# An attention and FFN layer on one core: the residual's DMA transposes move from ScalarE's queue to the sync queue

## The chip, the cores and the metric

One core of a Trainium2 chip runs the whole layer in one launch. The metric is the device time of one execution in microseconds; lower is better. Five engines run their own programs in order and meet through semaphores: TensorE (PE), VectorE (DVE), ScalarE (ACT), GpSimd (POOL) and SyncE (SP). DMAs are issued here by SP and by ACT, each from its own queue, in the order of its program.

## The reference

```python
def reference(x, wq, bq, wk, bk, wv, bv, wl, bl, w1, w2, w3):   # x: (1, 2048, 1024) f32
    h = layernorm(x)
    q, k, v = (h @ w.T + b for each of the three, as (S, 32 heads, 32))
    scores = einsum('bshd,bstd->bsht', q, k) / sqrt(32)     # over the heads of ONE token
    x = x + einsum('bsht,bstd->bshd', softmax(scores), v)
    h = layernorm(x)
    dq1, dq2, dq3 = nf4_quant_dequant(w1), ...(w2), ...(w3)   # w1, w2: (2752, 1024), w3: (1024, 2752)
    return x + (silu(h @ dq1.T) * (h @ dq2.T)) @ dq3.T
```

Attention mixes the 32 heads within each token, so each token has its own 32x32 score matrix. The latent projection of the original is computed there and not used. nf4_quant_dequant rounds each weight, divided by the largest magnitude of its block of 64, to one of 16 levels.

## The kernel before, in words

The tokens are cut into T = 16 tiles of 128. The first 105 us or so load and split the three projection weights into two f16 halves (wT_hi, wT_lo). Then the attention runs as a software pipeline of steps n = 0 to 15, and from about 570 us the FFN takes over. Steps 2 to 13 are a hardware loop of six rounds with two steps each, u = 0 for even n and u = 1 for odd n. Steps 14 and 15 are written out, and a tail finishes the last two tiles while the FFN's first units begin ("feed").

In step n the work of three tiles is mixed. Tile n is projected to q, k and v. Tile n-1 gets its attention: its scores are 64 small f32 matmuls between the projection's matmuls of 512 columns, with the block-diagonal q_diag as weights, and its mix is another 64, with p_diag as weights. Tile n-2 gets its end: context, residual, second norm and transpose.

PE in step n: the first projection with the scores (project_one with score_part), the turn of tile n+1, the second projection, and the third with the mix (mix_part) inside its last half. 24 matmuls of 512 columns carry the scores, 16 carry the mix. score_part waits for q_placed, k_ready and ctx_read: the last says that weigh has read the previous context out of the two banks that scores and context share.

VectorE in step n (step at line 755): weigh(n-2), which waits for the mix; one evacuation; the statistics; flip_context; turn_v; norm_apply; look 1; moments2; two evacuations; center (the row maximum of the scores); norm2; the low half of the turned x; flip_probs; the row sums; look 2; the transpose of q; look 3; an evacuation; look 4; an evacuation; the transpose of k; look 5; the last evacuation. A "look" (look_at, L752) takes the block maxima of one 512 KB slice of an FFN weight in ff_raw, which has two slots. A step with u = 0 has five looks, one with u = 1 has four, step 14 has six, step 15 none. The list for a step is `todo`, and SP loads by the same list.

The part that the change touches is the end of tile n-2:

1. VectorE: norm2 writes the normed rows into x_res (L857).
2. ScalarE: halve2 writes the f16 high half to x2_half (L952), after the previous tile's two transposes (x2_turned).
3. A DMA transpose, x2_half to x2_hi (turn_high2, L597). It also waits until the previous tile's x2_hi and x2_lo are stored (x2_out).
4. POOL: low2 writes the f16 low half into x2_half (L709), once that transpose has landed.
5. A DMA transpose, x2_half to x2_lo (turn_low2, L602), after low2 (x2_lo_done).
6. SP: store_x2 stores both to DRAM (L649), once both have landed. load_res loads the next tile's rows into x_res (L255) after low2.

SP's program for a step is: load_x (L252); the first load of todo (load_ff, L611 or L613); store_x1 (L643), which waits for POOL's residual; loads 2 to 4 of todo; load_res after low2; the loads from the fifth on (`todo[4:]`); store_x2. Each load_ff waits until the look two loads earlier has freed its slot of ff_raw (for the first of each round, until the look just before). In step 15 SP also issues the loads of the FFN's first weights, after parts of the projection.

ScalarE's program for a step is: split_hi, exponential, halve2, turn_high2, place_probs (four copies that make p_diag, L908), turn_low2, place of q_diag (four copies). In the tail the transposes of the last two tiles are issued by SP already.

Of the kernel before, what the change touches and what calls it, by code (L numbers as in the profile page):

```python
# [182 lines left out]
def attention(nc, g):  # L183
# [13 lines left out]
    with ExitStack() as mine:  # L197
# [53 lines left out]
        def load_x(sp, n, slot):  # L251
            sp.dma_start(x_nat[:, slot], x_dram[bass.ds(n * P, P), :]).then_inc(x_in[slot], 16)  # L252

        def load_res(sp, n):
            sp.dma_start(x_res[:], x_dram[bass.ds(n * P, P), :]).then_inc(res_in, 16)  # L255
# [265 lines left out]
        projected = sem("projected")  # L521
# [59 lines left out]
        def looks(n, u, it):  # L581

            if it is not None:
                places = [u * IN_LOOP[0] + k for k in range(IN_LOOP[u])]
                return [(it * 3 + 2 + q // 3, q % 3, it * 9 + 6 + q, P, q % 2, it * (5, 4)[q % 2] + 3 + q // 2 + 1, 1 + (q == 0))
                        for q in places]
            if n < 2:
                return [(j // 3, j % 3, j, P, j % 2, j // 2 + 1, 1) for j in range(3 * n, 3 * n + 3)]
            first = 6 + 9 * LOOP
            return [(j // 3, j % 3, j, P if j < 3 * FT else REST, (j + 1 - first) % 2, (5, 4)[(j + 1 - first) % 2] * LOOP + 3 + (j - first) // 2 + 1, 1)  # L590
                    for j in range(first, first + 6)] if n == T - 2 else []

        def turn_high2(eng, n):
            eng.wait_ge(x2_out, 32 * (n + 1))
            eng.wait_ge(x2_hi_done, n + 1)
            eng.sem_inc(held, 1)
            eng.dma_start_transpose(x2_hi[:], x2_half[:]).then_inc(x2_turned, 16)  # L597

        def turn_low2(eng, n):
            eng.wait_ge(x2_lo_done, n + 1)  # L600
            eng.sem_inc(held, 1)
            eng.dma_start_transpose(x2_lo[:], x2_half[:]).then_inc(x2_turned, 16)  # L602

        def sync(sp, feed):
            def load_ff(tile, m, j, rows, slot, times, behind):
                first = tile * P
                sp.wait_ge(absmax_done, j + behind)
                if m == 2:
                    sp.sem_inc(held, 1)
                if m < 2:  # L610
                    sp.dma_start(ff_raw[0:rows, slot], (w1, w2)[m][bass.ds(first, rows), :]).then_inc(ff_in[slot], 16)  # L611
                else:
                    sp.dma_start(ff_raw[:, slot, 0:C * rows].rearrange("p (t h) -> p t h", t=C),  # L613
                                 w3.rearrange("(t p) h -> p t h", p=P)[:, :, bass.ds(first, rows)]).then_inc(ff_in[slot], 16)

            def step(n, u, it, project=True, normalize=True, attend=True, end=True, feed=None):
                todo = looks(n, u, it)
                if normalize and not (it is None and n + 2 >= T):
                    sp.wait_ge(x_turned, 2 * n + 2)
                    load_x(sp, n + 2, u)  # L620
                for look in todo[:1]:
                    load_ff(*look)
                if end:
                    store_x1(n - 2)
                if feed:
                    sp.wait_ge(projected, 6 * n + 2)
                    next(feed)
                for look in todo[1:4]:
                    load_ff(*look)
                if end and attend:  # L630
                    sp.wait_ge(x2_lo_done, n - 1)
                    load_res(sp, n - 1)
                if feed:
                    sp.wait_ge(projected, 6 * n + 4)
                    next(feed)
                for look in todo[4:]:
                    load_ff(*look)
                if end:
                    store_x2(n - 2)

            def store_x1(n):
                sp.wait_ge(res_done, n + 1)
                sp.dma_start(x1_dram[bass.ds(n * P, P), :], x_res[:]).then_inc(x1_out, 16)  # L643

            def store_x2(n):
                sp.wait_ge(x2_turned, 32 * (n + 1))
                sp.sem_inc(held, 1)
                for dram, part in ((x2_hi_dram, x2_hi), (x2_lo_dram, x2_lo)):
                    sp.dma_start(dram[bass.ds(n * P, P), :], part[:].rearrange("p c s -> p (c s)")).then_inc(x2_out, 16)  # L649

            def tail(feed):
                sp.wait_ge(projected, 6 * T)
                sp.wait_ge(evacuated, 6 * T)
                sp.wait_ge(x2_out, 32 * (T - ST_BLOCK + 1))
                next(feed)
                store_x1(T - 2)
                sp.wait_ge(q_placed, T)
                sp.wait_ge(v_ready, T)
                sp.wait_ge(x2_turned, 32 * (T - 2))
                next(feed)  # L660
                next(feed)
                turn_high2(sp, T - 2)
                sp.wait_ge(x2_lo_done, T - 1)
                load_res(sp, T - 1)
                turn_low2(sp, T - 2)
                store_x2(T - 2)
                next(feed)
                store_x1(T - 1)
                next(feed)
                next(feed)  # L670
                turn_high2(sp, T - 1)
                turn_low2(sp, T - 1)
                store_x2(T - 1)

            sp.wait_ge(projected, 1)
            load_res(sp, 0)
            sp.sem_inc(x2_out, 32)
            all_steps(sp, step, tail, feed)
            sp.wait_ge(x1_out, 16 * T)
            sp.wait_ge(x2_out, 32 * (T + 1))  # L680
# [223 lines left out]
        def scalar(act, feed):  # L904
            def place(diag, compact, done):

                for rows in quadrants:
                    last = nc.scalar.activation(diag[rows, :, rows], compact[rows].rearrange("p (t h) -> p t h", h=HEADS), ACT.Copy)  # L908
                last.then_inc(done, 1)

            def step(n, u, it, project=True, normalize=True, attend=True, end=True, feed=None):
                if normalize:
                    split_hi(act, n + 1, xT_hi[:, 1 - u], x_turned, x_hi_done)
                if attend:
                    exponential(n)
                if end:
                    halve2(n - 2)
                    turn_high2(act, n - 2)
                if attend:
                    place_probs(n, end)  # L920
                if feed:
                    next(feed)
                if end:
                    turn_low2(act, n - 2)
                if project:
                    act.wait_ge(q_ready, n + 1)
                    if attend:
                        act.wait_ge(scores_done, n)
                    else:
                        act.wait_ge(diag_zero, 1)  # L930
                    place(q_diag, qT[:].rearrange("p t h -> p (t h)"), q_placed)
                if feed:
                    next(feed)

            def exponential(n):
                act.wait_ge(centered, n)
                flat = probs[:].rearrange("p t h -> p (t h)")
                nc.scalar.activation(flat, flat, ACT.Exp, scale=float(1 / np.sqrt(np.float32(HD)))).then_inc(exp_done, 1)

            def place_probs(n, end):  # L940
                act.wait_ge(p_ready, n)
                if end:
                    act.wait_ge(context_done, n - 1)
                else:
                    act.wait_ge(diag_zero, 2)
                place(p_diag, flipped[:], p_placed)

            def halve2(n):
                act.wait_ge(normed2, n + 1)
                if not (isinstance(n, int) and n == 0):  # L950
                    act.wait_ge(x2_turned, 32 * n)
                nc.scalar.activation(x2_half[:], x_res[:], ACT.Copy).then_inc(x2_hi_done, 1)  # L952

            def tail(feed):
                next(feed)
                exponential(T)
                next(feed)
                place_probs(T, True)
                next(feed)
                halve2(T - 2)  # L960
                next(feed)
                halve2(T - 1)

            all_steps(act, step, tail, feed)

        def tensor(pe, feed_program):
# [891 lines left out]
```

## Time and profile before

| | |
|---|---|
| median of 3 runs | 2005.99 us (2005.11 to 2007.31) |
| the profiled execution, its own time | 2009.52 us |
| its span in the trace | 2007.6 us |
| mean granted TensorE clock | 0.987 of full speed |
| one loop step (weigh to weigh) | 32.6 us |

The profile is of one execution. Times in rows are us from the start of its span, durations of single instructions are in us in a timeline and in ns where a mean is given. A row of a timeline has the start, the busy time, the engine, the line of the kernel, the operation, and what it writes and reads. "[1.54 <-DMA ff_raw...]" says that the engine stood idle for 1.54 us before it and what ended that. "SPq" and "ACTq" are DMA issues on the queues of SP and ACT; the data lands later. "PEclk" is the granted TensorE clock as a share of 2.4 GHz.

### The profile page before, as it was taken

What the parts mean: (1) busy time and instruction counts of PE and PEld (TensorE: products, weight loads), DVE (VectorE), ACT (ScalarE), POOL (GpSimd) and SP (SyncE); (2) the same over time, 40 slices, a digit from 0 to 9 for tenths busy, and PEclk for the clock granted to TensorE, in tenths of its full rate; (3) what the DMA queues carried; (4) which work ended last, traced back from release to release, by engine and by line L of the source; (5) the groups of instructions that cost most, each with busy time, mean ns of one, the idle gap of its engine ahead of it and who ended that gap; (6) DMA issues with size and microseconds to landing.
All of it is one profiled execution on the core that took longest, in us unless ns stands there. A gap on an engine that the chain in (4) does not pass through costs nothing. (4 is left out here: it accounts for less than half of the span.)

```text
span 2007.6 us, 30891 instructions
## 1 busy us (share of the span) xinstructions
PE 1964.3 (98%) x10444; PEld 1070.1 (53%) x10444; DVE 1784.9 (89%) x1789; ACT 1456.1 (73%) x1592; POOL 1189.5 (59%) x713
## 2 busy tenths in 40 slices
PE   6999999999999989999999999999999999999998
PEld 6678777777775434444444444444444444444442
DVE  6788898989877899999999999999999999999982
ACT  7242424233365889989899898998989989898882
POOL 0111111111133778787787877878778787886974
PEclk9999999999977999999999999999999999999999
DMA  7235555464445632221212122121222212122114
GB/s 304 94 93 158 149 157 162 131 167 141 127 146 153 225 90 59 48 58 42 63 42 63 42 47 57 42 63 42 53 51 45 59 42 63 42 48 53 38 28 177
DMA packets 253418, 183.77 MB, mean 92 GB/s; under 512 B 177456, under 2 KB 220464, under 8 KB 253360
## 3 DMA queue, kind: packets, MB, share of 16 engines
q1 hardware_dynamic: 223792, 175.67, 31.3%
q10 hardware_dynamic: 29568, 7.34, 2.1%
q8 instruction: 34, 0.56, 0.1%
q14 instruction: 24, 0.20, 0.0%
HBM read 115.34 MB, written 25.17 MB: 70 GB/s over the span
## 5 line engine op out<-in xcount | busy, mean ns | idle before, releaser
L1587 DVE SCALAR_TENSOR_TENSOR bank<-signs,bank 128x1024 f32<-128x1024 int8 (+2 forms) x761 | 926.5, 1217 | 53.9 <-ACT signs L1451 25.8
L1451 ACT ACTIVATE signs<-w_nat,compare_bias 128x1024 int8<-128x1024 f32 (+2 forms) x896 | 959.2, 1133 | 5.1 <-POOL w_nat L1335 1.3
L1758 PE MATMUL bank<-x2T_hi,w12T_hi 128*128 128x512 f16 x1376 | 521.5, 379 | 2.1 <-DVE w_nat L1604 1.3
L1759 PE MATMUL bank<-x2T_lo,w12T_hi 128*128 128x512 f16 x1376 | 521.5, 379 | 0.0
L1760 PE MATMUL bank<-x2T_hi,w12T_lo 128*128 128x512 f16 x1376 | 521.5, 379 | 0.0
L985 PE MATMUL bank<-wT_hi,xT_hi 128*128 128x512 f16 x768 | 294.0, 383 | 2.4 <-PEq L324 2.4
L985 PE MATMUL bank<-wT_hi,xT_lo 128*128 128x512 f16 x768 | 294.3, 383 | 0.0
L1785 PE MATMUL bank<-w3T_hi,hT_hi 128*128 128x512 f16 x672 | 255.7, 380 | 8.5 <-DMA w3T_lo<-half 5.8
L1787 PE MATMUL bank<-w3T_hi,hT_lo 128*128 128x512 f16 x672 | 255.4, 380 | 0.0
L1786 PE MATMUL bank<-w3T_lo,hT_hi 128*128 128x512 f16 x672 | 255.3, 380 | 0.0
L1377 POOL TENSOR_TENSOR acc<-acc,hidden 128x512 f32<-128x512 f32 x176 | 221.0, 1270 | 45.7 <-ACT hidden L1500 44.9
L1347 POOL TENSOR_SCALAR step_part<-w_nat 128x1024 f32<-128x1024 f32 (+1 forms) x64 | 230.5, 3602 | 14.3 <-POOL w_nat L1360 7.4
L1758 PEld LDWEIGHTS bank<-x2T_hi,w12T_hi 128*128 128x128 f16 x1376 | 134.6, 98 | 165.1 <-DVE w_nat L1604 1.8
L1760 PEld LDWEIGHTS bank<-x2T_hi,w12T_lo 128*128 128x128 f16 x1376 | 134.6, 98 | 162.4
L1759 PEld LDWEIGHTS bank<-x2T_lo,w12T_hi 128*128 128x128 f16 x1376 | 134.6, 98 | 162.1
L1356 POOL TENSOR_TENSOR w_nat<-w_nat,step_part 128x1024 f32<-128x1024 f32 (+1 forms) x64 | 149.7, 2339 | 101.5 <-DVE w_nat L1587 101.5
L1500 ACT ACTIVATE hidden<-bank,un_scale 128x512 f32<-128x512 f32 x176 | 120.2, 683 | 116.2 <-PE bank L1787 60.7
L290 ACT ACTIVATE xT_hi<-bank 128x512 f16<-128x512 f32 x32 | 17.4, 594 | 245.4 <-PE bank L284 245.4
L274 POOL TENSOR_TENSOR rstd<-var_eps,power 128x1 f32<-128x1 f32 x16 | 8.8, 552 | 275.7 <-DVE var_eps L266 275.7
L1029 PEld LDWEIGHTS bank<-vT,p_diag 128*128 128x128 f32 x1024 | 157.1, 208 | 17.0 <-ACT p_diag L908 8.4
L1666 DVE SCALAR_TENSOR_TENSOR acc<-bank,un_scale,acc 128x512 f32<-128x512 f32 x176 | 131.4, 746 | 38.7 <-PE bank L1783 28.4
L1019 PEld LDWEIGHTS bank<-kT,q_diag 128*128 128x128 f32 x1024 | 156.1, 191 | 11.8 <-issue 0.3
(141 smaller groups left out, 2720.0 us busy)
## 6 DMA issues: line engine op xcount, KB each, us to landing
ff_raw<-in_L_ffn_w SPq DMA_DIRECT2D x63, 512.0 KB, 4.4
w_nat<-in_L_ffn_w SPq DMA_DIRECT2D x63, 512.0 KB, 3.8
x_nat<-in_L_attn_hidden_states SPq DMA_DIRECT2D x16, 512.0 KB, 3.9
x_res<-in_L_attn_hidden_states SPq DMA_DIRECT2D x16, 512.0 KB, 4.9
x<-x_res SPq DMA_DIRECT2D x16, 512.0 KB, 3.0
acc<-x SPq DMA_DIRECT2D x4, 2048.0 KB, 8.7
out<-acc SPq DMA_DIRECT2D x16, 512.0 KB, 2.6
w_raw<-in_L_attn_wq SPq DMA_DIRECT2D x8, 512.0 KB, 7.3
```

The costliest lines, as they stand in the source:

```text
L985: ins = nc.tensor.matmul(to, x, w, start=j == 0, stop=j == len(passes) - 1)
L1029: ins = nc.tensor.matmul(context[:, t], p_diag[:, t], vT[:, t], start=True, stop=True)
L1347: nc.gpsimd.tensor_scalar(step_part[0:rows, 0:cols], w_nat[0:rows, slot, 0:cols], float(BOUNDS[APART]), 2 * HALF_STEP[APART], ALU.is_gt, A ...
L1377: nc.gpsimd.tensor_tensor(acc[:, st, BANK:], acc[:, st, BANK:], hidden[:, st % 2], ALU.add).then_inc(summed, 1)
L1451: nc.scalar.activation(signs[0:rows, ring(v, k), 0:cols], w_nat[0:rows, v % SLOTS, 0:cols], ACT.Sign, scale=COMPARE[SUMMED[k]][0], bias=co ...
L1587: V.scalar_tensor_tensor(to, part, HALF_STEP[SUMMED[k]], before, ALU.mult, ALU.add).then_inc(sign_used, 1)
L1758: nc.tensor.matmul(dst, hi, x2T_hi[:, toks, c], start=c == 0, stop=False)
L1759: nc.tensor.matmul(dst, hi, x2T_lo[:, toks, c], start=False, stop=False)
L1760: last = nc.tensor.matmul(dst, lo, x2T_hi[:, toks, c], start=False, stop=c == C - 1)
L1785: nc.tensor.matmul(dst, hT_hi[k, p, toks], w3T_hi[k, p, cols], start=p == 0, stop=False)
L1786: nc.tensor.matmul(dst, hT_hi[k, p, toks], w3T_lo[k, p, cols], start=False, stop=False)
L1787: last = nc.tensor.matmul(dst, hT_lo[k, p, toks], w3T_hi[k, p, cols], start=False, stop=p == GROUP - 1)
```

## The change

The two DMA transposes of tile n-2 in steps 2 to 15 are no longer issued by ScalarE but by SP. In SP's program the high one stands behind loads 2 to 4 of todo, and the low one behind load_res, ahead of `todo[4:]`. In step 15, where SP also serves the FFN, load_res stands behind the second of the FFN's loads instead of ahead of it. The tail stays as it is, and no computation changes.

```diff
--- before.py
+++ after.py
@@ -627,12 +627,16 @@
                     next(feed)
                 for look in todo[1:4]:
                     load_ff(*look)
+                if end:
+                    turn_high2(sp, n - 2)
+                if feed:
+                    sp.wait_ge(projected, 6 * n + 4)
+                    next(feed)
                 if end and attend:
                     sp.wait_ge(x2_lo_done, n - 1)
                     load_res(sp, n - 1)
-                if feed:
-                    sp.wait_ge(projected, 6 * n + 4)
-                    next(feed)
+                if end:
+                    turn_low2(sp, n - 2)
                 for look in todo[4:]:
                     load_ff(*look)
                 if end:
@@ -915,13 +919,10 @@
                     exponential(n)
                 if end:
                     halve2(n - 2)
-                    turn_high2(act, n - 2)
                 if attend:
                     place_probs(n, end)
                 if feed:
                     next(feed)
-                if end:
-                    turn_low2(act, n - 2)
                 if project:
                     act.wait_ge(q_ready, n + 1)
                     if attend:
```

The two helpers that are called are unchanged:

```python
        def turn_high2(eng, n):
            eng.wait_ge(x2_out, 32 * (n + 1))
            eng.wait_ge(x2_hi_done, n + 1)
            eng.sem_inc(held, 1)
            eng.dma_start_transpose(x2_hi[:], x2_half[:]).then_inc(x2_turned, 16)
```

turn_low2 waits for x2_lo_done alone and writes x2_lo.

## Rows read from the trace of the kernel before

**Rows 1.** The page, busy time and share of the span for each engine.
```profile
PE 1964.3 (98%) x10444; PEld 1070.1 (53%) x10444; DVE 1784.9 (89%) x1789; ACT 1456.1 (73%) x1592; POOL 1189.5 (59%) x713
```

**Rows 2.** Timeline of PE and its weight loads: first of mix, first of scores.
```profile
340.57 0.56 PEld L1029 LDWEIGHTS bank<-vT,p_diag 128*128 128x128 f32 x4 [0.19 <-ACT p_diag L908]
...
351.72 0.30 PE L1019 MATMUL bank<-kT,q_diag 128*128 128x32 f32 x2
```

**Rows 3.** Timeline of VectorE and POOL: looks, low2 and weigh of two loop steps.
```profile
337.27 1.21 DVE L752 TENSOR_REDUCE absmax<-ff_raw 128x1024 f32 x1
338.08 2.13 POOL L709 TENSOR_TENSOR x_half<-x_res,x_half 128x1024 f16<-128x1024 f32 x1 [8.40 <-DMA x_hi<-x_half]
...
342.04 1.22 DVE L752 TENSOR_REDUCE absmax<-ff_raw 128x1024 f32 x1
...
347.46 1.22 DVE L752 TENSOR_REDUCE absmax<-ff_raw 128x1024 f32 x1 [1.54 <-DMA ff_raw<-in_L_ffn_w]
...
350.07 1.23 DVE L829 TENSOR_TENSOR probs<-bank,inv_sum 128x1024 f32<-128x1024 f32 x1 [0.73 <-PE bank L1029]
...
382.70 1.23 DVE L829 TENSOR_TENSOR probs<-bank,inv_sum 128x1024 f32<-128x1024 f32 x1 [2.68 <-PE bank L1029]
...
391.34 1.21 DVE L752 TENSOR_REDUCE absmax<-ff_raw 128x1024 f32 x1
```

**Rows 4.** Timeline of ScalarE in the step of rows 2.
```profile
333.79 1.04 ACT L952 ACTIVATE x_half<-x_res 128x1024 f16<-128x1024 f32 x1
334.92 1.25 ACTq L597 DMA_TRANSPOSE x_hi<-x_half  x1
336.27 4.25 ACT L908 ACTIVATE p_diag<-flipped 32x1024 f32<-32x1024 f32 x4 [1.44 <-DVE flipped L865]
340.31 1.25 ACTq L602 DMA_TRANSPOSE x_lo<-x_half  x1
```

**Rows 5.** Timeline of SP's queue: three loads of the loop, two issues of the tail.
```profile
338.66 0.33 SPq L611 DMA_DIRECT2D ff_raw<-in_L_ffn_w  x1
...
341.43 0.33 SPq L611 DMA_DIRECT2D ff_raw<-in_L_ffn_w  x1
...
381.68 0.35 SPq L611 DMA_DIRECT2D ff_raw<-in_L_ffn_w  x1
...
621.95 0.50 SPq L1245 DMA_DIRECT2D w_nat<-in_L_ffn_w  x1
622.58 1.24 SPq L597 DMA_TRANSPOSE x_hi<-x_half  x1
```

**Rows 6.** DMA issues, last number us to landing: whole kernel, then 615 to 640.
```profile
x_hi<-x_half ACTq DMA_TRANSPOSE x14, 3.1
...
w_nat<-in_L_ffn_w SPq DMA_DIRECT2D x1, 512.0 KB, 4.8
...
x_hi<-x_half SPq DMA_TRANSPOSE x1, 5.0
```

**Rows 7.** Timeline of PE: first matmul of the last two mixes.
```profile
571.40 0.79 PE L1029 MATMUL bank<-vT,p_diag 128*128 128x32 f32 x4 [3.04 <-ACT p_diag L908]
...
615.54 0.41 PE L1029 MATMUL bank<-vT,p_diag 128*128 128x32 f32 x2 [1.92 <-ACT p_diag L908]
```

**Rows 8.** Windows: length, PE busy (matmuls), granted clock, DMA share, GB/s.
```profile
340.70:350.00 9.30, 9.30 (x82) 1.00 0.95 262
351.70:361.90 10.20, 10.20 (x89) 1.00 0.32 107
571.40:588.80 17.40, 17.40 (x79) 0.51 0.45 106
588.80:592.20 3.40, 3.40 (x10) 0.50 0.03 8
615.50:634.70 19.20, 18.38 (x83) 0.52 0.53 110
634.70:640.00 5.30, 5.30 (x15) 0.50 0.73 229
```

## The prediction

> **What bounds the kernel now.** I read the page first, then the timeline of a loop step engine by engine, then PE's waits around the two places where it needs other engines, and last the landing times of the transposes. PE is busy for 98% of the span [rows 1]: whatever makes PE stand is paid in full, and what frees another engine is worth only the standing of PE that it ends.
>
> In a loop step PE runs the scores inside the first projection, then turns x, projects twice more with the mix inside the last half, and goes on to the next step. In the stretches of the mix and of the scores it is busy without a gap [rows 8]. It needs p_diag for the mix, and there the weight load waited 0.19 us for it; it needs weigh(n - 2), which frees the scores' banks, at 351.72, the first score [rows 2].
>
> The margin that matters is VectorE's before that score. weigh starts at 350.07 and lasts 1.23 us, to 351.30: 0.42 us before PE asks. In the steps with u = 0 a fifth look at a slice of FFN weights stands ahead of weigh. It starts at 347.46 after 1.54 us of waiting for its DMA; VectorE then idles 0.73 us before weigh [rows 3]. So that load may land 0.73 + 0.42 = 1.15 us later, at about 348.6, before PE stands. With u = 1 there is no fifth look, and VectorE idles 2.68 us before weigh [rows 3].
>
> **What the change takes from ScalarE.** Two DMA issues of 1.25 us per step [rows 4]. The first stands between x_half and p_diag: p_diag starts at 336.27, the transpose ends at 334.92 + 1.25 = 336.17, and flip_probs ends a little earlier, so I estimate p_diag 0.1 to 0.3 us sooner. PE can get back at most the 0.19 us of the weight load in each of 13 steps, 2.5 us; part of that is covered by the matmul still running. In step 15 PE stands 3.04 us for p_diag [rows 7], and there the transpose costs it up to 1.25 us. The second transpose stands before q_diag, which PE needs only for the next step's scores. Together between 0 and 3.7 us of gain; I take 1, mostly step 15.
>
> **What it does to the sync queue.** SP issues in order. The high transpose now stands behind todo[1:4], the low one behind POOL's low2 and load_res, and todo[4:], the load of that fifth look, behind both. With x_half ready at 334.83 (333.79 + 1.04) [rows 4], a step with u = 0 goes so:
>
> The last load of todo[1:4] is issued at 338.66, after the look at 337.27 has freed its slot [rows 3, 5]. The high transpose follows at about 339.1, not at 334.92. It lands 5.0 us later if it behaves as the SP transpose at 622.58, which also stands 0.6 us behind a 512 KB load; as ScalarE's it would take 3.1 [rows 5, 6]. The situation is that of the row with 5.0, so I take it: 344.1.
>
> POOL's low2 takes 2.13 us [rows 3]: 346.3. Then load_res at 346.4, the low transpose from 346.8 to 348.05, and the load of the fifth look at 348.15 instead of 341.43 [rows 5]. (I count 0.33 us for issuing a load and 0.1 us between two issues, as between x_half's end and its transpose.) It lands 4.8 us later if like the 512 KB load at 621.95, which has transposes ahead of it [rows 6]: 352.95. The look moves by 5.5 us; less 1.15, PE stands 4.4 us before the scores.
>
> The bounds: the fastest landings are 3.1 us for a transpose and at most 3.4 for a load (338.66 to the look at 342.04, which did not wait) [rows 3, 5, 6]; they give an issue at 346.25, a look at 349.65 and a stand of 1.0 us. The slowest is the 6.0 us from issue to look of this very load now (341.43 to 347.46): a stand of 5.6 us. No stand at all would need a landing 2.3 us after its issue.
>
> The Trainium skill, page "DMA: Bandwidth & Descriptors", section "Issuing engines are not separate DMA queues", speaks against a landing that depends on the queue: DMAs of all issuers interleave on the same 16 engines, and another issuer saves only the time of issuing. By that the high transpose would land in 3.1 us and PE would stand 2.5 us; the row at 622.58 shows 5.0.
>
> This happens in six loop steps (n = 2, 4 to 12) and in n = 14, where two loads stand behind the transposes; I give it the same price. 7 x 4.4 = 31 us.
>
> In steps with u = 1 no load waits behind the low transpose of the step itself. Counted from their scores, which come 32.6 us later, the high transpose goes out at about 371.7, the low one lands at 384, and the stores of x2 and the load of x_nat follow; the first load of the next step is issued at about 386 instead of 381.68, lands at 390.8, and VectorE looks at 391.34 [rows 3, 5]. It just fits. I price it at 0; the upper bound is 1 us in each of six steps.
>
> The rest on SP has cover: the residual behind load_res waits for flip_context, which comes after weigh and moves with it; x_nat is needed a whole step later; nobody in the loop waits for the stores of x2 but the next x2_half. In step 15 the third load of w_nat gets ahead of the wait for low2.
>
> **The clock.** A stand of PE has a second price here. In step 15 PE stood 3.04 us ahead of a mix. The mix then ran at a granted clock of 0.51, that is at 1.2 GHz, and took 17.4 us for what the loop does in 9.3 us at 2.4 GHz, and the clock stayed low for 3.4 us of plain 512-column matmuls behind it. In the last mix PE stood 1.92 us; that mix too ran at 0.52 to its end, and 5.3 us more at 0.50 [rows 7, 8]. Stands of 4.4 us are longer than both. If the scores, 10.2 us now, stay low as these mixes did, they cost 10.2 x (17.4 / 9.3 - 1) = 8.9 us more, and the matmuls behind them lose half of 3.4 to 5.3 us, I take 2.2: 11.1 us per stand, 7 x 11.1 = 78 us. The bounds of the term are 0 and 8.9 + 2.65 = 11.6. Its weak point: scores are denser in 512-column matmuls than mixes (24 instead of 16, beside 64 small ones), and the clock may come back within them. The nearest row is the mix, so I take 11.1.
>
> The Trainium skill, page "TensorE: Matmul & The Clock Gate", section "HAM oscillation — how this bites in real kernels", has a loop in which PE waits in every round pay the warm-up in every round. By that the low clock comes back seven times, and the trace's two stands agree so far as they go.
>
> **Sum.** 31 + 78 - 1 = +108 us. The profiled execution took 2009.52 us with a span of 2007.6; the median of the runs is 2005.99, 3.5 us less. I put the difference on the median: 2114 us.
>
> **The rivals.**
> 1. *PE stands, but the clock holds or is back within a few us.* For it: the scores are denser, and the loop's mix keeps 1.00 [rows 8]. 31 to 31 + 7 x 4 = 59 us: 2036 to 2065. Chance 0.25.
> 2. *The chain on SP is quick.* Stands of 1 to 2 us, too short for the clock: +7 to +14 us, 2013 to 2020. Against it: the landing of 5.0, and 1.92 us was not too short. Chance 0.08.
> 3. *No change.* SP spends most of a step waiting, 2.5 us more of issue vanish in that, and no look is late: 2003 to 2010. It decides if the load of the fifth look lands by 348.6 instead of 353. Against: the order on SP. Chance 0.09.
> 4. *Faster.* In step 15 p_diag comes 1 us sooner, PE stands 2 us instead of 3.04, and the clock stays up: 17.4 - 9.3 + 1.7 + 1 = 11 us less, 1995. It decides if 2 us is too short for the fall, which 1.92 us was not in the last mix; and no look may be late. Chance 0.05.
>
> **The numbers.** My forecast (stands, low clock through the scores) has 0.50; its own range is 2085 to 2140, from stands of 3 to 5.6 us and 2 us either way in the clock's term. Above 2140 lies 0.03. The range of 2015 to 2140 holds the forecast, rival 1 and most of rival 2. A measurement of this kernel can tell about 0.2%, 4 us, from no change. Faster by more than that is rival 4, 0.05; within it is rival 3, 0.09; slower is the rest, 0.86.
>
> **What would show it.** In the changed profile the fifth look (L752 with u = 0) waits for the DMA of ff_raw for 5 to 8 us instead of 1.54; ahead of the first score of steps 3, 5 to 15 PE is idle some 4.4 us, released by weigh; two loop steps take about 81 us instead of 65 (70 if the clock holds); the granted clock in the page's slices falls below full speed all through the loop; the high transpose is issued 0.1 to 0.5 us behind a load of ff_raw, and lands in 4 to 5 us; p_diag starts at the end of flip_probs. I am wrong if low2 starts before 342 on this time scale, if the fifth load lands before 349, or if the clock of the scores behind a stand reads 1.00.

## The result and the profile after

The changed kernel takes 2095.52 us (median of 4 runs, 2094.47 to 2096.67) against 2005.91 us (4 runs as well): a ratio of 1.0443 with an interval of 1.0431 to 1.0456, 4.4% slower, where 2114 was forecast. Its profiled execution took 2095.57 us with a span of 2093.8.

The changed kernel, timeline of SP's queue, one round of the loop from the third load of a step with u = 0 (it answers to [rows 5]):
```profile
381.37 0.33 SPq L611 DMA_DIRECT2D ff_raw<-in_L_ffn_w  x1
381.90 1.24 SPq L597 DMA_TRANSPOSE x_hi<-x_half  x1
388.38 0.34 SPq L255 DMA_DIRECT2D x_res<-in_L_attn_hidden_states  x1
388.96 1.24 SPq L602 DMA_TRANSPOSE x_lo<-x_half  x1
390.39 0.65 SPq L611 DMA_DIRECT2D ff_raw<-in_L_ffn_w  x1
```
The third load is at 381.37 and the fifth at 390.39, 9.0 us apart; before it was 2.8 us. Between them stand the transpose, low2 and the next transpose.

Timelines of VectorE, POOL and PE in the same stretch ([rows 3] and [rows 2]):
```profile
386.03 2.14 POOL L713 TENSOR_TENSOR x_half<-x_res,x_half 128x1024 f16<-128x1024 f32 x1 [13.65 <-DMA x_hi<-x_half]
...
394.87 1.22 DVE L756 TENSOR_REDUCE absmax<-ff_raw 128x1024 f32 x1 [5.82 <-DMA ff_raw<-in_L_ffn_w]
396.01 0.74 DVE L742 SCALAR_TENSOR_TENSOR qkv<-bank,scales,bias 128x512 f32<-128x512 f32 x1
396.67 1.21 DVE L833 TENSOR_TENSOR probs<-bank,inv_sum 128x1024 f32<-128x1024 f32 x1
...
398.03 0.61 PE L1020 MATMUL bank<-kT,q_diag 128*128 128x32 f32 x2 [3.42 <-DVE probs L833]
```
The fifth look waits 5.82 us for its load instead of 1.54. weigh follows the evacuation without a gap, so it no longer waits for PE, and PE stands 3.42 us for it. The list of who waited for weigh counts seven such stands, 24.5 us in all, the longest 4.5.

Windows of PE in the changed kernel: length, PE busy, granted clock ([rows 8]). The first three are the stand, the scores after it, and the start of the plain matmuls behind; the last is the mix of step 15.
```profile
395.00:398.00 3.00, 0.00 (x0) 1.00 0.93 278
402.00:417.90 15.90, 15.90 (x72) 0.50 0.29 99
417.90:421.00 3.10, 3.10 (x13) 0.50 0.00 0
421.00:425.00 4.00, 4.00 (x18) 0.88 0.00 0
...
666.40:675.60 9.20, 9.20 (x80) 1.00 0.48 145
```
The scores run at half clock to their end and take 19.96 us here (398.03 to 417.99) instead of 10.3. The clock returns about 4 us into the plain matmuls here; behind the other six passes it took 1.1 to 3.3 us. One reading went the other way: the mix of step 15, at 0.51 before, keeps 1.00.

### The profile page after: what moved, and what is told of

Read it like the earlier page. It is cut to its first block and busy times, and to the rows that moved or that the text cites. A ratio compares the mean times of both kernels' runs of the same rounds, so it can differ in the third digit from the quotient of the medians.

```text
span 2093.8 us, 30879 instructions
## 1 busy us (share of the span) xinstructions
PE 2021.8 (97%) x10444; PEld 1113.7 (53%) x10444; DVE 1783.2 (85%) x1789; ACT 1456.3 (70%) x1592; POOL 1189.5 (57%) x713
## 5 line engine op out<-in xcount | busy, mean ns | idle before, releaser
L986 PE MATMUL bank<-wT_hi,xT_hi 128*128 128x512 f16 x768 | 312.6, 407 | 2.4 <-PEq L324 2.4
L986 PE MATMUL bank<-wT_hi,xT_lo 128*128 128x512 f16 x768 | 313.1, 408 | 0.0
L1348 POOL TENSOR_SCALAR step_part<-w_nat 128x1024 f32<-128x1024 f32 (+1 forms) x64 | 230.5, 3602 | 14.3 <-POOL w_nat L1361 7.4
L1020 PEld LDWEIGHTS bank<-kT,q_diag 128*128 128x128 f32 x1024 | 208.4, 247 | 48.3 <-issue 28.0
L1020 PE MATMUL bank<-kT,q_diag 128*128 128x32 f32 x1024 | 183.1, 288 | 24.5 <-DVE probs L833 24.5
L713 POOL TENSOR_TENSOR x_half<-x_res,x_half 128x1024 f16<-128x1024 f32 x16 | 34.2, 2137 | 247.2 <-DMA x_hi<-x_half 247.2
```

The lines of the kernel that those rows point to most:

```text
L986: ins = nc.tensor.matmul(to, x, w, start=j == 0, stop=j == len(passes) - 1)
L1020: ins = nc.tensor.matmul(scores[:, t], q_diag[:, t], kT[:, t], start=True, stop=True)
L1348: nc.gpsimd.tensor_scalar(step_part[0:rows, 0:cols], w_nat[0:rows, slot, 0:cols], float(BOUNDS[APART]), 2 * HALF_STEP[APART], ALU.is_gt, A ...
```

## The experiments

Unless the text names another base, each is an edit of the changed kernel. Stands and lengths of scores and mixes are read from the timelines of PE.

**The fifth load ahead of the transposes' chain.**
```diff
+                for look in todo[4:]:
+                    load_ff(*look)
                 if end and attend:
                     sp.wait_ge(x2_lo_done, n - 1)
                     load_res(sp, n - 1)
                 if end:
                     turn_low2(sp, n - 2)
-                for look in todo[4:]:
-                    load_ff(*look)
```


> The changed kernel with one swap in SP's program: the loads from the fifth on (todo[4:]) stand ahead of load_res and the low transpose. Theory A (the loss is the fifth load's place in SP's order; PE stands for the fifth look, and the clock falls on the stand): the load goes out at about its old time, 2.7 us after the fourth, the fifth look waits under 2.7 us, no PE idle ahead of the scores, granted clock 1.00 through the loop, two loop steps in 65.3 us. Median 1996 to 2007 us: 2006 if nothing else is left, down to 1996 if p_diag of step 15 comes 1 us sooner and PE's short stand there leaves the clock up. Theory B (the transposes on SP's queue are themselves the cost, by landing later and crowding the loads): the high transpose still lands in 4 to 5 us behind the load, low2 is as late as in the changed kernel, and a good part of the loss stays: above 2040 us.

Measured: 2005.68 us, ratio 0.9991 (0.9982 to 1.0001). Both transposes are still on SP's queue. SP's queue in this kernel:
```profile
338.33 0.33 SPq L611 DMA_DIRECT2D ff_raw<-in_L_ffn_w  x1
338.88 1.24 SPq L597 DMA_TRANSPOSE x_hi<-x_half  x1
341.07 0.34 SPq L611 DMA_DIRECT2D ff_raw<-in_L_ffn_w  x1
345.32 0.33 SPq L255 DMA_DIRECT2D x_res<-in_L_attn_hidden_states  x1
345.77 1.25 SPq L602 DMA_TRANSPOSE x_lo<-x_half  x1
```
load_res and the low transpose are 5 us later than in the kernel before, and nobody misses them. No stand is left in the loop, and VectorE idles 2.10 us before weigh. The whole loss came from the fifth load's place in the order (in step 14 two loads stand there), and theory B falls.

In step 15 PE stood 1.94 us for p_diag instead of 3.04, and the mix still ran at half clock, 17.2 us: ScalarE's relief takes 1.1 us off that stand, too little to show in the kernel's time (the interval of the ratio holds 1), and the clock was not kept across a stand of 1.9 us.

**Only the high transpose on SP.** ScalarE issues turn_low2 as before.
```diff
                 if feed:
                     next(feed)
+                if end:
+                    turn_low2(act, n - 2)
                 if project:
```
(a part of the edit; the call on SP is taken out)

> Only the high transpose is issued by SP, the low one by ScalarE as before. Theory A: low2 and with it load_res are as late as in the changed kernel, and the fifth load waits behind load_res, only 1.4 us sooner than there (the low transpose's issue). The fifth look waits some 4.5 us for its DMA, PE stands 2 to 3 us ahead of the scores seven times, the clock falls as in the changed kernel: 2070 to 2095 us. A theory by which only the issue time of the two transposes on SP counts (2.5 us per step) would give about half of the loss, 2050. By the theory that the clock wants a stand of over 3 us: stands without a fall, 2006 + 7 x 2.5 = 2024 us.

Measured: 2097.73 us, ratio 1.0454 (1.0438 to 1.047): the whole loss. Seven stands, 3.2 to 5.2 us, 26.7 us in all; all seven passes of scores at low clock. I had expected 2 to 3 us of stand, because the fifth load goes out 1.4 us sooner. It does, 7.7 us behind the third, but it then takes 5.7 us to land instead of 4.3: ScalarE's queue issues the low transpose at 390.05, 0.7 us ahead of the load at 390.79. The likely reason is that the two share the DMA engines; no run tests it by itself. What costs the loss is low2 being late with the load behind it, and not the issue time of two transposes. The theory of stands over 3 us was not tested here, since no shorter one was left.

**Only the low transpose on SP.** The high one stays with ScalarE, behind halve2.

> Only the low transpose is issued by SP, the high one by ScalarE as before. Theory A: low2 ends at its old time, load_res goes out at its old time, and the fifth load only 0.8 us later than before (the low transpose's issue stands ahead of it), which is inside the margin of 1.15 us before weigh: no stand, 2002 to 2009 us. If the fifth load behind the transpose's data on the same queue lands later than now (over 6.3 us): stands of about 1 us and, if the clock falls on them, up to 2080. Theory B: part of the loss, about 2040.

Measured: 2006.37 us, ratio 1.0 (0.999 to 1.0009). VectorE around the fifth look:
```profile
348.03 1.22 DVE L754 TENSOR_REDUCE absmax<-ff_raw 128x1024 f32 x1 [1.75 <-DMA ff_raw<-in_L_ffn_w]
349.17 0.74 DVE L740 SCALAR_TENSOR_TENSOR qkv<-bank,scales,bias 128x512 f32<-128x512 f32 x1
350.43 1.23 DVE L831 TENSOR_TENSOR probs<-bank,inv_sum 128x1024 f32<-128x1024 f32 x1 [0.52 <-PE bank L1029]
```
The idle time before weigh shrinks from 0.73 to 0.52 us and absorbs it. The two halves of the change are not alike: the low one costs nothing that these runs can tell, the high one carries the loss.

**The kernel before, with only the load's place changed.** No transpose moves.
```diff
-                for look in todo[4:]:
-                    load_ff(*look)
                 if end:
                     store_x2(n - 2)
+                for look in todo[4:]:
+                    load_ff(*look)
```


> The kernel before, transposes on ScalarE's queue, with one swap in SP's program: todo[4:] stands behind store_x2. The fifth load then goes out at about 347.2 instead of 341.4 on the scale of the trace of before, nearly as late as in the changed kernel (48.2). Theory A: the fifth look waits 5 to 6 us, PE stands 3 to 4 us seven times, the clock falls on each: 2085 to 2110 us, as slow as the changed kernel or slower, though no transpose has moved. Theory B: about 2006 us.

Measured: 2086.45 us, ratio 1.0406 (1.0378 to 1.0433). The loss without the change: the fifth load goes out 8.95 us behind the third, the look waits 6.09 us, and PE stands seven times, 22.8 us in all. Here two of the seven kept the clock. PE's timeline at the first of the two:
```profile
554.01 0.38 PE L1019 MATMUL bank<-kT,q_diag 128*128 128x32 f32 x2 [2.87 <-DVE probs L829]
```
and the windows of the scores of both (length, PE busy, granted clock):
```profile
554.00:564.30 10.30, 10.29 (x88) 1.00 0.24 82
...
621.90:632.20 10.30, 10.26 (x88) 1.00 0.13 52
```
The second of them followed a stand of 2.29 us. The five others, of 3.0 to 4.3 us, were followed by scores of 18.9 to 19.9 us.

**PE kept at work in the stand.** In steps with u = 1, PE runs 13 matmuls with unused results ahead of the wait.
```diff
+                    if first == 0 and end and u == 1:
+                        fill(13)
                     score_part(n, end, first, last)
...
+            def fill(count):
+                for _ in range(count):
+                    nc.tensor.matmul(bank[:, TURN], xT_hi[:, 1, 0], wT_hi[:, 0, 0, 0:BANK], start=True, stop=True)
```


> The changed kernel, and in each step with u = 1 PE runs 13 matmuls of 512 columns with unused results ahead of its wait for the scores, 2.8 us of the 3.0 to 4.5 us that it stood there. Theory A (the low clock comes from the stand): remaining stands of 0.2 to 1.7 us, scores at clock 1.00 in 10.3 us instead of 18.6 to 20.0. Seven times 9.0 us for the scores and 1.3 for what follows is 72 us less: 2024 us, and up to 2040 if the mixes of the tail, which the changed kernel runs at full clock, stand for p_diag again as in the kernel before. Theory C (the clock falls for another reason than the stand, as the sparser matmuls of mix and scores, or the stand does not matter at all): 2090 us or more, with scores still at 0.50.

Measured: 2031.87 us, ratio 1.0142 (1.0107 to 1.0177), 64 us less than the changed kernel for useless work. PE's timeline at the first filling, and then the window of the scores behind it:
```profile
293.14 2.97 PE L1016 MATMUL bank<-wT_hi,xT_hi 128*128 128x512 f16 x13
297.30 0.38 PE L1026 MATMUL bank<-kT,q_diag 128*128 128x32 f32 x2 [1.19 <-DVE probs L833]
```
```profile
297.30:307.60 10.30, 10.30 (x88) 1.00 0.34 114
```
PE still can't begin the scores before weigh, but stands only 0.4 to 1.2 us of that time, and all seven passes of scores take 10.4 us at full clock. Fill and rest of stand, 7 x 2.8 + 5.7 = 25.3 us, are the 25.1 us by which it is slower than the kernel before on the same chip (2031.87 against 2006.79). So the stands by themselves cost some 25 us, and the rest of the loss is the clock. In step 15 of this kernel the scores come at full clock, and PE stands for p_diag again; its timeline and the window of that mix:
```profile
596.23 0.91 PE L1036 MATMUL bank<-vT,p_diag 128*128 128x32 f32 x4 [2.23 <-ACT p_diag L912]
```
```profile
596.20:613.90 17.70, 17.67 (x80) 0.51 0.26 76
```

**With 6 instead of 13.**

> As the run with 13, but 6 such matmuls, 1.3 us: stands of 1.7 to 3.2 us are left. Two stands of 2.3 and 2.9 us ahead of scores kept the clock in the run with only the load's place changed, while 1.5 and 1.9 us ahead of a mix brought it down. If stands under some 3 us keep the clock ahead of scores: nearly as the run with 13, 2024 to 2045 us. If they bring it down as ahead of a mix: 2085 to 2096 us. A mixture is possible, since stands of about 3 us went both ways.

Measured: 2095.04 us, ratio 1.0427 (1.0404 to 1.0449): nothing gained. The stands left were of 1.97 to 3.21 us, and each was followed by scores of 18.4 to 20.0 us, as in this row of PE's timeline and the window behind it:
```profile
318.23 0.38 PE L1026 MATMUL bank<-kT,q_diag 128*128 128x32 f32 x2 [2.23 <-DVE probs L833]
```
```profile
318.20:337.20 19.00, 18.97 (x88) 0.53 0.31 104
```
A stand of 2.23 us brings the clock down here, where 2.29 and 2.87 us did not two runs above. The length of a stand alone does not decide it.

**Filling the stand of step 15**, on top of the load moved ahead.
```diff
                 if first == 0:
+                    if isinstance(n, int) and n == T - 1:
+                        fill(8)
                     pe.wait_ge(p_placed, n)
```


> The version with the load moved ahead (2005.7 us), and in step 15 PE runs 8 unused matmuls of 512 columns, 1.7 us of its stand of 1.9 us, ahead of its wait for p_diag. Theory A: the mix of step 15 keeps the clock and takes 9.2 us instead of 17.2, PE is 8 us sooner there. If nothing else is bound in the tail: 1997 us. If the FFN's first codes on VectorE and ScalarE are what ends last there, PE stands for them a little later and gets back only part: 2000 to 2005 us. If the clock falls all the same: 2006 us.

Measured: 2000.39 us, ratio 0.9967 (0.9955 to 0.9979), faster than both kernels. The mix takes 9.3 us at clock 1.00, after a stand of 0.20 us. PE then stands 3.7 us behind it, at the FFN's first sums: part of the 8 us is given back at once, as expected. Against the version with the load moved ahead it is 5 us faster, by the two ratios to the kernel before (0.9967 and 0.9991, whose intervals do not meet).

**Filling the last mix's stand too**, with two f32 matmuls (1.7 us).

> As the run before it, and two f32 matmuls of 512 columns with unused results ahead of the last mix's wait for p_diag (stand of 1.5 us). They take 0.9 us each at full clock. If the clock holds through the last mix too: up to 8 us less than the run with one filling, 1990 to 2000 us. If the standing for the FFN's first codes inside that mix brings it down anyway, or if these matmuls count for nothing: as that run, or 0.5 us slower.

Measured: 2001.38 us, ratio 0.9968 (0.9956 to 0.998), the same as the run before. The windows of the last mix, first with one filling, then with both:
```profile
608.80:626.70 17.90, 16.64 (x85) 0.61 0.53 118
```
```profile
611.50:621.30 9.80, 9.80 (x85) 1.00 0.70 135
```
The mix is 8 us shorter and the kernel is not. PE's waits from the end of that mix to 750 us, first with one filling (all of them), then with both (one of 0.6 us is left out):
```profile
PE bank L1792 <- DMA w3T_lo<-half: 4.6, 1, 4.6
PE bank L1765 <- DVE w_nat L1611: 1.3, 1, 1.3
PE bank L1765 <- DMA w12T_lo<-half: 1.0, 1, 1.0
```
```profile
PE bank L1769 <- DMA w12T_lo<-half: 6.2, 2, 3.3
PE bank L1796 <- DMA w3T_lo<-half: 4.7, 1, 4.7
PE bank L1769 <- DVE w_nat L1615: 3.0, 1, 3.0
PE bank L1769 <- DVE hidden L1624: 1.5, 1, 1.5
```
PE waits 6.9 us there with one filling and 16.0 with both. What the clock gave, the FFN's first weights took back: there PE is no longer what ends last.

## Why the prediction was right, by its steps

**The order on SP.** Right as argued, and shown from both sides: with the load moved ahead the loss is gone with both transposes on SP, and with the load moved back it comes without them. What the prediction did not say is that the high transpose alone carries it.

**The size of a stand.** 4.4 us were predicted, 3.5 measured on average (24.5 / 7). The term that was too large is the landings: the high transpose took 4.1 us (median of the kernel 4.3) and not the 5.0 of [rows 6], and the load 4.3 and not 4.8. From the third load's issue to the fifth look's start it took 13.5 us (381.37 to 394.87), where the sum had 14.3. The prediction was wrong to set the 5.0 us against the page that it weighed (the Trainium skill, page "DMA: Bandwidth & Descriptors", section "Issuing engines are not separate DMA queues"). The page says that the DMAs of all issuers interleave on the same 16 engines, and not that a transpose lands in 3.1 us from any queue. The traces agree with it. DMA issues of the whole kernel before, with the median us to landing:
```profile
x_hi<-x_half ACTq DMA_TRANSPOSE x14, 3.1
x_lo<-x_half ACTq DMA_TRANSPOSE x14, 6.1
```
and the high transpose of step 15 of the changed kernel (655 to 665 us):
```profile
x_hi<-x_half SPq DMA_TRANSPOSE x1, 3.0
```
ScalarE's high transpose went out 7.4 us or more behind the last load. Its low one (340.31) stood between a load (338.66), load_res (340.43) and the fifth load (341.43), and took twice as long from the same queue. The one of SP in step 15, 6.9 us behind a load, landed as fast as ScalarE's high one. So the landing went with what else was in flight, and not with the queue. In steps 2 to 14 of the changed kernel, 0.5 to 0.7 us behind a load, it was 3.6 to 4.6 us: the row with 5.0 was the right kind of row, and too large by 0.7.

**Seven places, and none with u = 1.** Right: all seven stands are ahead of scores of odd steps.

**The clock.** The step with the weak point held. The scores were taken to stay low as the mixes had, at 19.1 us; they took 18.6 to 20.0 us in all seven cases. That they would was a choice between two values, which the rows of before, of mixes alone, could not settle. Up to the first score of step 15 PE is 635.73 - 547.49 = 88.2 us late: 24.5 us of stands, 54.8 us of six longer passes of scores, and 8.9 us left for the plain matmuls behind them, 1.5 us each where 2.2 was taken. That the clock is its own price, set off by the stand, is what the fillings with 13 and with 6 showed.

**ScalarE's relief and the tail.** This step was too small. It gave 1 us for step 15, and left the saving of the mix's low clock to the rival of a faster kernel. That gain came, inside the slower kernel: the mix of step 15 takes 9.2 instead of 17.6 us without a stand, the last mix 11.8 instead of 19.4. The start of the one mix is 95.1 us late, the end of the other 79.5. Of the 2.7 us by which p_diag comes sooner after its scores, 1.1 are the transpose's issue, and 1.6 are VectorE's: flip_probs starts 5.4 us after the end of the scores instead of 7.0. VectorE's work on the FFN's scales ends together with the scores before the change (557.78 and 557.79), and 8 us ahead of their end when these are slow (646.35 and 654.55). The runs bear out that this came with the slow scores. In the five kernels whose scores of step 15 ran at full clock and that have no filling ahead of this mix, PE stood 1.9 to 3.3 us for p_diag and the mix ran low; one of them is the changed kernel with 13 matmuls in its stands (2.23 us). In the three whose scores ran low there (the changed kernel, the high transpose alone on SP, the filling with 6) PE did not stand, and the mix kept the clock. In the FFN's opening PE then waits 8.4 us where it waited 2.1, and the end is 86.2 us late.

So in the spans +108 stood against +86.2. For the stands it had 31 where 24.5 were, for the clock 78 where it was 73.7 (54.8 and 8.9, and 8.5 and 1.5 for the seventh pass and the matmuls behind it), and for the tail -1 where it was the rest, 86.2 - 24.5 - 73.7 = -12. The tail is the largest of the three misses, 11 of 22 us.

**The rivals.** The clock did fall and stay (rival 1), the landings were not quick enough (rival 2), seven looks were late (rival 3). Rival 4's condition, 2 us being too short for the fall, did not hold in its own case: 1.94 us brought the mix down when only the load was moved ahead.

## What to carry to other kernels

When a DMA is moved to another in-order queue, list what is behind it there and ask what it waits for: a transfer that is itself not urgent delays the one behind it by its whole chain, here a transpose's landing, an engine's pass and another issue. Find the load whose consumer stands ahead of the bounding engine, and issue it first.

On a kernel bound by TensorE a short stand may cost far more than its length. Where it can't be removed, matmuls with unused results in it can be cheaper than standing: 2.8 us of them saved about 9 us here each time. The filling has to leave little of the stand: 1.3 us of it saved nothing.

## What the runs showed of the hardware

- A stand of PE ahead of sparse work (scores or mix, small f32 matmuls between those of 512 columns) was in most cases followed by the 1.2 GHz level, which set in at the latest 2.1 us into that work and held to its end, 16 to 20 us in all. Behind the scores it held for 1.1 to 4.1 us of plain 512-column matmuls more. Ahead of plain matmuls a stand of 2.3 us (after the mix of step 15 of the changed kernel) was followed by only 3.3 us at 0.50 (678.0 to 681.3).
- Of 28 stands of 1.97 us and more ahead of scores (four kernels), 26 were followed by the fall; 2.29 and 2.87 us in one kernel were not, while 1.97 us in another was. Ahead of mixes 1.52 to 3.33 us all were. Within the last mix, 1.88 us in the changed kernel was not, while 1.92 us in the kernel with 13 filling matmuls and 1.26 us in the one with 8 in step 15 were. Stands of 0.2 to 1.2 us directly ahead of scores or mixes never were. What decides between 1.2 and 2.9 us is left open.
- A transpose that went out with no load near it landed in 3.0 to 3.1 us from either queue. At 0.5 to 0.7 us behind a 512 KB load it took 3.6 to 4.6 us in the changed kernel; with one load 1.6 us ahead of it and another 0.1 us behind it, 5.7 to 6.5 us in the loop of the kernel before. A load issued 0.7 us behind a transpose on the other queue took 5.7 us, one 1.4 us behind a transpose on its own 4.3 us.
